# Vision transformer on one core: the first attention sums normalised tokens and applies Wv to the sums; five image buffers instead of six; semaphores per bank

## The reference, cut to what matters

```
tokens = patches @ W_map.T + b_map                  # 196 patches of 768 values -> 192
tokens = concat(class_token, tokens) + positions    # 197 x 192
x  = (tokens - mean) / sqrt(var + eps) * ln_w + ln_b   # mean and var over the whole image
q, k, v = x_h @ Wq.T + bq, x_h @ Wk.T + bk, x_h @ Wv.T + bv   # 12 heads of 16
att = softmax(q @ k.T / 4)                           # 197 x 197 for each head
h  = tokens + att @ v
...                                                  # causal attention, slots and experts, combine
```

## Time and profile before

| what | value |
|---|---|
| median of 3 runs | 4718.42 us (4712.15 to 4719.34) |
| the profiled execution | 4706.87 us |
| its span | 4705.1 us |
| TensorE (matmul) busy | 4417.1 us, 94% of the span |
| VectorE busy | 3407.1 us, 72% |
| ScalarE busy | 2723.7 us, 58% |
| GpSimd busy | 2053.1 us, 44% |
| data moved by DMA | 791.78 MB, mean 168 GB/s |

### The profile page before, as it was taken

One profiled execution on the slowest core, in us unless ns is written; L12 is line 12 of the kernel. 1 busy time (PEld: TensorE's weight loads), 2 busy tenths in 40 slices (PEclk: granted clock), 3 DMA queues, 4 the chain that ended last, 5 costly groups with the idle time before them and its releaser, 6 DMA issues. The chain is left out here.

```text
span 4705.1 us, 159457 instructions
## 1 busy us (share of the span) xinstructions
PE 4417.1 (94%) x47156; PEld 3827.4 (81%) x47156; DVE 3407.1 (72%) x10266; ACT 2723.7 (58%) x7054; POOL 2053.1 (44%) x3346
## 2 busy tenths in 40 slices
PE   8999999889999999999997999999999799989978
PEld 7999999867787777787776888888888576679965
DVE  5666666678787788887775888888887688830067
ACT  3444444356666666666664555555555699954445
POOL 2232232333333333443344666666666466631145
PEclk9999999979999999999997999999999799999955
DMA  5667776677777777776656777777774233369977
GB/s 171 191 194 192 193 194 191 177 161 172 168 171 169 170 170 168 180 173 165 164 137 147 159 159 159 161 158 160 158 160 110 69 96 95 96 184 276 271 212 230
DMA packets 459820, 791.78 MB, mean 168 GB/s; under 512 B 80443, under 2 KB 330748, under 8 KB 459644
## 3 DMA queue, kind: packets, MB, share of 16 engines
q1 hardware_dynamic: 459644, 789.24, 67.5%
HBM read 519.59 MB, written 265.72 MB: 167 GB/s over the span
## 5 line engine op out<-in xcount | busy, mean ns | idle before, releaser
L693 DVE TENSOR_REDUCE a_mx<-a_sq 99x2 f32<-99x394 f32 x1536 | 831.7, 563 | 244.9 <-PE a_sq L762 218.6
L642 ACT ACTIVATE a_ex<-a_sk 99x792 f32<-99x792 f32 (+1 forms) x768 | 639.7, 833 | 212.1 <-PE a_sk L776 196.8
L1174 DVE TENSOR_REDUCE c_mx<-c_sq 99x2 f32<-99x198 f32 (+1 forms) x1536 | 660.2, 457 | 28.1 <-PE c_sq L1243 16.0
L1133 ACT ACTIVATE c_ex<-c_sk 99x792 f32<-99x792 f32 (+1 forms) x768 | 512.1, 667 | 288.6 <-PE c_sk L1261 262.1
L1081 POOL TENSOR_SCALAR_AFFINE_SELECT c_ex<-c_ex 99x396 f32<-99x396 f32 (+1 forms) x768 | 422.2, 550 | 405.9 <-ACT c_ex L1133 401.2
L762 PE MATMUL a_sq<-a_ks,a_qs 96*99 96x198 bf16 x3072 | 545.7, 260 | 22.2 <-DMA a_ks<-scr_qk 17.7
L393 PE MATMUL e_tokp<-e_wmap,e_xin 128*99 128x192 f32 x3072 | 551.6, 330 | 14.0 <-DVE e_junk L341 14.0
L393 PEld LDWEIGHTS e_tokp<-e_wmap,e_xin 128*99 128x99 f32 x3072 | 483.4, 167 | 14.5 <-issue 14.0
L776 PE MATMUL a_sk<-a_qs,a_ks 99*99 99x198 bf16 (+1 forms) x3072 | 406.2, 255 | 44.5 <-issue 44.5
L1243 PE MATMUL c_sq<-c_ks,c_qs 96*99 96x99 bf16 (+1 forms) x3072 | 441.5, 231 | 0.0
L762 PEld LDWEIGHTS a_sq<-a_ks,a_qs 96*99 96x99 bf16 x3072 | 331.1, 130 | 112.8 <-DVE a_mx L693 51.5
(11 more groups left out here) (207 smaller groups left out, 10842.6 us busy)
## 6 DMA issues: line engine op xcount, KB each, us to landing
e_xin<-in_x SPq DMA_DIRECT2D x128, 594.0 KB
x_w<-in_fc SPq DMA_DIRECT2D x128, 576.0 KB, 5.6
scr_tv<-e_tv SPq DMA_DIRECT2D x128, 297.0 KB
a_tv<-scr_tv SPq DMA_DIRECT2D x128, 297.0 KB
scr_tv<-a_res SPq DMA_DIRECT2D x128, 297.0 KB
c_tv<-scr_tv SPq DMA_DIRECT2D x128, 297.0 KB
scr_qk<-e_parts SPq DMA_DIRECT2D x128, 222.8 KB
scr_qk<-e_parts SPq DMA_DIRECT2D x384, 74.2 KB
```

The lines of the kernel that those rows point to most:

```text
L642: nc.scalar.activation(ex[0:rows, g, kt].rearrange("p (a s) -> p a s", a=2), sk[k % 2][0:rows, :, 0:2 * SP], ACT.Exp).then_inc(exped.sem, 1)
L693: nc.vector.reduce_max(mx[:, b.parity, qt, h:h + 2], sq[f % 2][:, :, 0:SEQ], AX.X).then_inc(maxed.sem, 1)
L1133: nc.scalar.activation(to, of, ACT.Exp).then_inc(exped.sem, 1)
L1174: nc.vector.reduce_max(mx[:, b.parity, qt, h:h + 2], sq[f % 3][:, :, 0:SP if qt else TT], AX.X).then_inc(maxed.sem, 1)
```

## The change

- The embedding no longer makes values. The weights `e_wv`, the 12 matmuls of L434, the bias addition L380 and their events are gone. The normalised tokens are written straight into the second half of `e_tv`, which is stored as before, with the same number of bytes.
- Plain attention therefore sums normalised tokens, weighted by the exponentials. Wv and bv are put into a matrix `wv1` (128 x 3 x 68) that takes the place of the identity in `turn_sums`: an fp32 matmul with 68 columns replaces a transpose with 128. The row of bv meets the denominator, so that the division is right afterwards.
- R of plain attention is 5 instead of 6. Tiles that had two buffers by parity now have five, and waits on image b - 2 become waits on image b - R.
- `scored_q`, `maxed`, `scored_k` and `exped` become two events each, one for each PSUM bank. The second block of key scores has no wait of its own, and `value_products` waits once, for both exponentials, instead of once for each.
- In SP's step the six loads of queries and keys (L544) go from the front to the end, behind the maxima rows.

```
 embed_pass
-        xn = m.sb("e_xn", [TT, 2, 2, D])
-                    nc.vector.scalar_tensor_tensor(out=xn[:, w], in0=xc[:], scalar=st[:, w, 5:6], in1=lnb[:],
+                    nc.vector.scalar_tensor_tensor(out=tv[:, b2.place, 1], in0=xc[:], scalar=st[:, w, 5:6], in1=lnb[:],
-                    dve.wait_ge(v_done.sem, v_done.at(b3))
-                    nc.vector.tensor_tensor(tv[:, b3.place, 1], vp[:], bv[:].unsqueeze(1).broadcast_to([TT, 2, D]),
-                                            ALU.add).then_inc(v_copied.sem, 1)
-                    pe.wait_ge(v_copied.sem, v_copied.at(b3 - 1))
-                    for t in range(2):
-                        for g in range(3):
-                            for a in range(2):
-                                mm = nc.tensor.matmul(vp[:, t, g * 64:(g + 1) * 64], stack[:, b3.parity, g, t * TT:(t + 1) * TT],
-                                                      wvh[:, a, g], start=(a == 0), stop=(a == 1))
-                    mm.then_inc(v_done.sem, 1)
-                    sp.wait_ge(v_copied.sem, v_copied.at(b))
+                    sp.wait_ge(normed.sem, normed.at(b))
 attend_plain
-    R = 6
+    R = 5
-        mx = m.sb("a_mx", [TT, 2, 2, HEADS])
+        mx = m.sb("a_mx", [TT, R, 2, HEADS])
+        wv = m.sb("a_wv", [128, NG, G * (DH + 1)])
-        oT = (work[0:TT, 0:NG * 128], pvp[0:TT, 0:NG * 128])
+        oT = (work[0:TT, 0:HEADS * (DH + 1)], pvp[0:TT, 0:HEADS * (DH + 1)])
             def step(c):                               # SP
-                if c.inside(n):
-                    sp.wait_ge(scored_k.sem, scored_k.at(c - R))
-                    ...                                # the six loads L544
                 b = c - 1
                 if b.inside(n):
                     sp.wait_ge(added.sem, added.at(b - R))
                     sp.wait_ge(v_spread.sem, v_spread.at(b - R))
                     sp.dma_start(tv[:, b.place], scr["tv1"][b.number]).then_inc(tv_in_place.of(b), 16)
                 ...
+                if c.inside(n):
+                    sp.wait_ge(scored_k[1].sem, scored_k[1].at(c - R))
+                    ...                                # the six loads L544
             def key_scores(b, k):
-                if k < 2:
-                    pe.wait_ge(exped.sem, exped.at(b - 1, 5 + k))
-                else:
-                    pe.wait_ge(exped.sem, exped.at(b, k - 1))
+                if not kt:
+                    pe.wait_ge(exped[0].sem, exped[0].at(b, g))
             def value_products(b, g):
+                pe.wait_ge(exped[1].sem, exped[1].at(b, g + 1))
                 for kt in range(2):
-                    pe.wait_ge(exped.sem, exped.at(b, 2 * g + kt + 1))
             def turn_sums(b, t):
+                width = G * (DH + 1)
                 for g in range(NG):
-                    mm = nc.tensor.transpose(oT[t][:, g * 128:(g + 1) * 128], ot[:, b.parity, g, t * TT:(t + 1) * TT], ident[:])
+                    mm = nc.tensor.matmul(oT[t][:, g * width:(g + 1) * width], ot[:, b.place, g, t * TT:(t + 1) * TT], wv[:, g],
+                                          start=True, stop=True)
```

More of the change, by code:

```diff
@@ L252, in _ @@
                      (lnb[:], A["lnb"].rearrange("(t p) d -> p t d", p=TT)), (ident[:], A["ident"])]
-            loads += [(wqk[rows], A["wqk1"]) for rows in halves] + [(wv[rows], A["wv1"]) for rows in halves]
+            loads += [(wqk[rows], A["wqk1"]) for rows in halves]
             for e in (loaded, stored):
@@ L326, in _ @@
         def _(dve):
-            for e in (tokens, mean_s, rstd, centred, normed, x_low, v_copied, left):
+            for e in (tokens, mean_s, rstd, centred, normed, x_low, left):
                 e.seed(dve)
@@ L493, in attend_plain @@
         tv_in_place = m.transfers("a_tv_in_place")
-        scored_q = m.event("a_scored_q", 12)
-        maxed = m.event("a_maxed", 12)
+        scored_q = [m.event(f"a_scored_q{i}", 6) for i in range(2)]
+        maxed = [m.event(f"a_maxed{i}", 6) for i in range(2)]
         max_turned = m.event("a_max_turned")
@@ L502, in attend_plain @@
         v_spread = m.event("a_v_spread")
-        scored_k = m.event("a_scored_k", 6)
-        exped = m.event("a_exped", 6)
+        scored_k = [m.event(f"a_scored_k{i}", 3) for i in range(2)]
+        exped = [m.event(f"a_exped{i}", 3) for i in range(2)]
         summed = m.event("a_summed", 3)
@@ L597, in lower @@
                 m.hold(pool)
-                pool.tensor_copy(parts[:, b.parity, 1, chunk_of(i)], rest[:, chunk_of(i)]).then_inc(middle.sem, 1)
+                pool.tensor_copy(parts[:, b.place, 1, chunk_of(i)], rest[:, chunk_of(i)]).then_inc(middle.sem, 1)
                 pool.wait_ge(middle.sem, middle.at(b, i + 1))
-                pool.tensor_tensor(parts[:, b.parity, 2, chunk_of(i)], rest[:, chunk_of(i)],
-                                   parts[:, b.parity, 1, chunk_of(i)], ALU.subtract).then_inc(low.sem, 1)
+                pool.tensor_tensor(parts[:, b.place, 2, chunk_of(i)], rest[:, chunk_of(i)],
+                                   parts[:, b.place, 1, chunk_of(i)], ALU.subtract).then_inc(low.sem, 1)
             def step(c):
@@ L630, in _ @@
         def _(act):
-            for e in (exped, o_copied, h_copied, high, finished):
+            for e in (*exped, o_copied, h_copied, high, finished):
                 e.seed(act)
@@ L705, in split_rest @@
                 dve.wait_ge(low.sem, low.at(b - 1, i + 1))
-                nc.vector.tensor_tensor(rest[:, chunk_of(i)], qkp[:, 0:2 - i], parts[:, b.parity, 0, chunk_of(i)],
+                nc.vector.tensor_tensor(rest[:, chunk_of(i)], qkp[:, 0:2 - i], parts[:, b.place, 0, chunk_of(i)],
                                         ALU.subtract).then_inc(left.sem, 1)
@@ L2016, in lay_out @@
     bqk1 = np.zeros((2, DH, G, NG), np.float32)
-    wv1 = np.zeros((G, DH, NG, G, DH), np.float32)
+    wv1 = np.zeros((G, 32, NG, G, DH + 1), np.float32)
+    for r in range(G):
+        wv1[r, DH, :, r, DH] = 1.0
     for h in range(HEADS):
         g, r = h // G, h % G
+        j = h % G
         for i, (w, b) in enumerate((("Wq", "bq"), ("Wk", "bk"))):
```

106 lines of the change are left out of this document (53 added, 53 removed).

## The result

| | before | changed |
|---|---|---|
| median | 4715.28 us (4704.84 to 4719.34, 4 runs) | 4789.57 us (4773.05 to 4806.01, 4 runs) |
| ratio | | 1.0167 (95% interval 1.0144 to 1.0190) |
| span of the profiled execution | 4705.1 us | 4782.4 us |

What follows compares the result with a forecast made beforehand. It took a chain through three engines to bound the embedding, and TensorE plain attention, with stops at loop returns. Terms -60 - 70 + 70 = -60 us gave 4658 us from 4718.4, range 4615 to 4715 us.

Steps and rivals of the forecast that it cites:

- The embedding, -60 us: Embedding: dropping the values takes the bias addition off the limiting chain, 0.47 us for each of 128, -60 us.
- the ring: Embedding: chain round ScalarE, VectorE and TensorE said to set the pass; it loses only the bias addition, 0.47 us.
- TensorE's own shortening: Embedding: bound of 128 x 0.65 = -83 us if the three-engine chain were not what holds TensorE; no chance given.
- The stops of plain attention, -70 us: Plain attention: shorter loop no longer exceeds what TensorE keeps, so ten stops of 7.0 us at loop returns go.
- Causal attention, 0 us: Causal attention: code not touched, its loop taken to return without stopping, so no change in time.
- the stops stay: Plain attention rival, 8 in 100: loop returns still stop; 4742 us at the old rate, 4819 us if every return stops.
- The step of plain attention, 11.65 us: Plain attention: step grows from 11.10 to 11.65 us through turn_sums and later loads, 128 x 0.55 = +70 us.
- TensorE's part: Plain attention: fp32 matmuls in turn_sums add 0.4 to 0.64 us an image, making the step 11.5 to 11.74 us.
- The load chain: Plain attention: SP's six loads, issued late and needed two steps on, hold the step to 11.4 to 11.85 us.

Runs made afterwards that it cites:

- e8: Kernel before with the embedding's change alone, Wv and value bias left out, 194 semaphore increments ahead of plain attention; 4667.4 us, ratio 0.9903.
- e10: Kernel before with 75 increments ahead of the embedding, 151 of plain, 50 of causal attention, both loops inside seven blocks; 4647.7 us, ratio 0.9876.
- e1: Changed kernel with 142 do-nothing semaphore increments on TensorE ahead of causal attention, restoring its loop's place; 4643.3 us, ratio 0.9866.
- e2: Kernel before with 114 increments ahead of causal attention, putting its loop where the changed kernel has it; 4853.2 us, ratio 1.0304.
- e7: Changed kernel with the old transposes in turn_sums, Wv and value bias left out, 42 increments ahead of causal attention; 4619.2 us, ratio 0.9807.
- e6: Changed kernel with 142 increments spread over three passes and SP's six loads back at the front of its step; 4632.4 us, ratio 0.9834.
- e3: Kernel before with 256 increments, one whole block, ahead of causal attention; 4731.8 us, one execution.
- e11: As e10, with 10 more increments ahead of plain and 10 more ahead of causal attention; 4770.2 us, one execution.
- e5: Changed kernel with 142 increments split 48, 47, 47 over the starts of embedding, plain and causal attention; 4648.4 us, ratio 0.9861.
- e4: Kernel before with 128 increments ahead of plain and 128 ahead of causal attention; 4749.5 us, one execution.
- e9: Kernel before with 218 increments ahead of plain and 16 ahead of causal attention, both loops at remainder 193; 5060.2 us, one execution.

## Why the prediction was wrong, step by step

*The embedding, -60 us: right.* -57.6, by the mechanism named: 0.45 us an image where 0.47 was forecast, the bias addition out of the ring. e8 gives 55.1 for that part alone. The rival there, TensorE's own shortening, would have been 83.

*The stops of plain attention, -70 us: right in the result, half right in the reason.* They are gone, and they were worth 76 us (the steps of the kernel before beyond 11.10 us, summed) or 77 (e10). The reason given was length alone, by a count of matmuls and weight loads (1,596): "the plain loop lies just beyond what TensorE keeps". With the other instructions it has 1,786, or 6.98 blocks, and the causal one 6.82, and e10 runs the longer of them without a stop. What decides is whether the loop fits into seven blocks where it lies. The new plain loop has 5.82 (1,491 instructions) and fits anywhere, so the forecast came out.

*Causal attention, 0 us: this is the step that failed.* The prediction took "returns to without stopping" as a property of the causal loop, and of its 1,560 instructions, and costed only the passes that the diff touches. It is a property of its place. Its 1,747 instructions (waits and all) fit into seven blocks from 46 of 256 places; it was in one, and taking 398 instructions out ahead of it moved it to one of the other 210. It cost 144 us where the sum had nothing, more than twice the 67 us gained in the changed passes. e1 and e2 show it from both sides.

*The stops as a rival:* "the stops stay" had the size nearly right (7 us a stop; 19 x 7.6 in the event) and the wrong loop. The prediction's trace had the warning in it: loops of 6.98 and 6.82 blocks, one with stops and one without, is a margin that shouldn't be believed to hold when code ahead of it moves.

*The step of plain attention, 11.65 us: too high by 0.13.* TensorE's part was forecast at +0.4 to +0.64 us, and measured +0.35 (11.45), below the range. The six loads take 0.60 us against 0.36, 0.24 more for each half, but in the starts of the matmuls the halves cost only 0.17 and 0.22 us more (from the first record to the next block 0.57 and 0.47 us in e6, 0.40 and 0.25 in e10), and a block behind them gives 0.04 back. The load chain was forecast at 11.4 to 11.85 and is 11.43 (e7). Together the mean is 11.52. In the sum, for plain attention: -76 (stops) + 45 (128 x 0.35) + 9 (loads just in time) + 13 (next) = -9 us, as measured. Without the stops these terms and the embedding's -57.6 come to +9 us: the rest of the change gained nothing.

*A term that wasn't there.* Two of the first steps take 15.09 and 18.13 us (before, 11.80 and 11.16), 10.3 us more; with 2.6 us more up to the first L813, where TensorE waits 3.2 us for loads in SP's new order (e6, in the old one, 1.3), that is some 13 us. In the two steps TensorE is busy throughout, at the lower clock. The changed kernel's stretches, 60 to 75 us after the pass's first product:

```profile
955.00:960.00 5.00, 5.00 (x38) 3.84 (x36) 2.81 (x7) 2.14 (x5) 0.00 (x0) 0.50 0.01 3
960.00:965.00 5.00, 5.00 (x39) 3.86 (x39) 1.95 (x5) 1.64 (x3) 1.67 (x3) 0.56 0.23 64
965.00:970.00 5.00, 5.00 (x63) 4.40 (x62) 4.06 (x10) 3.49 (x6) 2.58 (x6) 1.00 0.80 165
```

The kernel before, 42 to 47 us after its first product:

```profile
995.00:1000.00 5.00, 4.70 (x61) 3.13 (x49) 3.43 (x9) 2.80 (x6) 1.00 (x1) 0.91 0.05 13
```

The clock comes up 69 us after the start; before it was 43 us, and in e7, which differs from the changed kernel only by the old transposes as far as this pass goes, 47.5. e6 has the same slow steps (15.09 and 17.94) with SP's old order, so it is `turn_sums` and not the loads. All four profiles with six fp32 records for three transposes have 68 to 72 us, all nine with transposes 40 to 48. Why the records keep the clock down longer wasn't tried.

*What stays open.* That an eighth block makes TensorE fetch all of them again is read from the packets: 167, less the 7 to 13 of a stretch without stops, are 8.1 to 8.4 for each of the 19 returns. How the memory chooses what to drop isn't shown. Nor is why a few instructions in the eighth block stop a third or half of the returns and 86 or more stop all.

The Trainium skill, page "Runtime: NRT & Kernel Launch", section "Instruction fetch mechanics", gives TensorE 2048 instructions in a first-in-first-out memory, filled in blocks of 256. The blocks of 256 agree with e3 and e10, and eight blocks, one of them ahead of use, would leave seven for a loop, which would explain what e10 and e11 show; that one is kept ahead is my reading. By capacity alone the loop before, with 1,786 instructions, would have fitted wherever it lay, and it stopped. Its sentence that a taken branch outside "the current 2-page window" stalls doesn't hold here: e10 returns over seven blocks 38 times without a stop.

## What to carry to other kernels

In this kernel a long loop on TensorE returned without a stop only where it lay inside seven whole blocks of 256 instructions, and an edit ahead of it that does no work cost 3% (e2) or gave 3% back (e1). So after a change look at the instruction queue's packets and the "issue" waits of every loop, the untouched ones first, and compare passes one by one before judging the edit by the total. Where they show stops, shorten the loop to six blocks (then it lies inside seven anywhere), or move it by a few idle instructions placed where the engine waits anyway. A trial of an edit is only fair when both versions have their loops in good places: here that is 4643 or 4648 us (e1, e5) against 4648 (e10), nothing gained, and 4632 (e6) once SP's new order is undone; as first measured it was 4790 against 4715.

## What the runs showed of the hardware

- A stop at a return costs 7.6 us in causal attention (143.9 / 19) and 7.7 in plain attention (77.4 / 10), of which 4 to 5 are idle and the rest is work at 1.2 GHz behind it. In e11 it is 8.1 and 8.4 us, and in e4, where every return of plain attention stops, 5.6: (1595.2 - 1477.8 - 10.8) / 19, where 10.8 us are the increments ahead of causal attention.
- A return with a second block to fetch costs 10.5 us (e9: 1677.9 - 1477.8 = 200.1 us in 19 returns of plain attention). I had expected 4875 for e9 with stops in causal attention and got 5060.
- A semaphore increment takes 0.156 us on TensorE, and some 60 of them vanish behind the 17 us in which causal attention waits for its first loads (e1, e2, e3).
- The clock stays at the lower level for 40 to 48 us from plain attention's first product with transposes in `turn_sums` and for 68 to 72 with fp32 matmuls, which is worth some 10 us. In causal attention it is 27 to 28 us in most profiles, 18 to 20 where 114 or more increments stand ahead of the first product, and 52 to 54 in e5 and e8.
